# Selective-state mixer and expert layer on one core: projecting B and C before the output, and taking the key/query norm's power before a block's deviation

## The reference, cut to what matters

```
Bn = B * rsqrt(mean(B*B) + 1e-5) * B_norm_w          # C alike
K  = rope(Bn + B_bias, theta)   # 4 heads x 128; Q from C, theta = cumsum(angles * dt)
y_intra = (Q K^T * decay mask) @ x ;  y_inter = Q @ state ;  state = fade*state + K^T x
out = ((y_intra + y_inter + D*x) * silu(z)) @ W_out
```

## Time and profile before

| | |
|---|---|
| median of 3 runs | 280.01 us (279.19 to 280.21) |
| profiled execution | 278.36 us, span 276.6 us |
| TensorE busy | 248.3 us (90%) |
| VectorE busy | 223.8 us (81%) |
| GpSimd busy | 208.3 us (75%) |
| ScalarE busy | 149.2 us (54%) |
| granted TensorE clock, mean | 0.969 |

### The profile page before, as it was taken

One profiled execution on the slowest core, in us unless ns is written; L12 is line 12 of the kernel. 1 busy time (PEld: TensorE's weight loads), 2 busy tenths in 40 slices (PEclk: granted clock), 3 DMA queues, 4 the chain that ended last, 5 costly groups with the idle time before them and its releaser, 6 DMA issues.

```text
span 276.6 us, 7390 instructions
## 1 busy us (share of the span) xinstructions
PE 248.3 (90%) x2155; PEld 218.4 (79%) x2158; DVE 223.8 (81%) x607; ACT 149.2 (54%) x508; POOL 208.3 (75%) x291
## 2 busy tenths in 40 slices
PE   2999997599999999999999999999999999999600
PEld 0857964488997999899889979997999899889400
DVE  4768998988878969896989698788969896987446
ACT  1765989555365453745364645456453755372033
POOL 8658997858788888788887888888788876675400
PEclk9999999799999999999999999999999999999955
DMA  5540827976869888987897688969878997770096
GB/s 157 195 129 11 298 86 219 303 202 207 265 192 270 275 246 239 289 264 208 261 293 263 216 248 262 316 196 269 276 239 253 275 268 248 231 236 21 21 274 181
DMA packets 68855, 61.55 MB, mean 222 GB/s; under 512 B 6608, under 2 KB 52304, under 8 KB 68816
## 3 DMA queue, kind: packets, MB, share of 16 engines
q1 hardware_dynamic: 66256, 55.83, 66.3%
q0 software_dynamic: 2560, 5.25, 6.3%
HBM read 56.27 MB, written 4.78 MB: 221 GB/s over the span
## 4 chain that ended last, share of the span: by engine, by line
PE 72%; DVE 10%; ACT 6%; POOL 4%; DMA 3%; issue 3%; SPq 1%; POOLq 0%; ACTq 0%; DVEq 0%
PE bank L877 20%; PE bank L922 9%; PE bank L872 5%; PE bank L820 5%; PE bank L812 5%; PE bank L836 3%; PE bank L797 3%; PE bank L767 3%; PE bank L804 2%; PE bank L772 2%; PE bank L854 2%; PE bank L845 2%; PE bank L918 2%; DMA decay<-res_dram 2%; PE bank L863 2%
## 5 line engine op out<-in xcount | busy, mean ns | idle before, releaser
L877 PE MATMUL bank<-blkT,w_up 128*128 128x128 f32 x512 | 64.4, 279 | 1.2 <-ACT blkT L1091 1.2
L877 PEld LDWEIGHTS bank<-blkT,w_up 128*128 128x128 f32 x512 | 61.8, 195 | 2.0 <-issue 1.3
L637 POOL DMA_INDIRECT res_dram<-xrow,sidx x40 | 40.7, 1018 | 22.0 <-DVE xrow L1423 17.7
L583 POOL DMA_INDIRECT blk<-xn_dram,gidx x40 | 42.1, 1052 | 8.7 <-issue 7.6
L922 PE MATMUL bank<-w,xrow 128*128 128x128 f32 x256 | 34.7, 278 | 0.3 <-DVE xrow L1410 0.3
L922 PEld LDWEIGHTS bank<-w,xrow 128*128 128x128 f32 x256 | 31.1, 192 | 1.6 <-issue 1.6
L1327 DVE SCALAR_TENSOR_TENSOR kq<-sd,rms,bias_kq 128x512 f32<-128x512 f32 x32 | 23.5, 772 | 10.6 <-POOL rms L594 9.8
L1097 ACT ACTIVATE xrow<-bank 128x512 f32<-128x512 f32 x40 | 24.6, 614 | 13.6 <-PE bank L877 13.6
L1395 DVE TENSOR_TENSOR xrow<-xrow,bank 128x512 f32<-128x512 f32 x40 | 27.1, 678 | 0.6 <-PE bank L877 0.6
L630 POOL TENSOR_TENSOR rstd<-mv,mhalf 128x1 f32<-128x1 f32 x40 | 25.2, 629 | 1.5 <-DVE mv L1407 1.3
L1060 ACT ACTIVATE kqT<-bank 128x512 f32<-128x512 f32 x16 | 9.6, 597 | 27.3 <-PE bank L797 27.3
(11 more groups left out here) (246 smaller groups left out, 620.6 us busy)
## 6 DMA issues: line engine op xcount, KB each, us to landing
w_up<-in_L_ffn_W_dram SPq DMA_DIRECT2D x96, 256.0 KB
w<-in_L_ffn_W_dram SPq DMA_DIRECT2D x48, 256.0 KB, 4.4
e_row<-e_dram SPq DMA_DIRECT2D x16, 256.0 KB, 4.2
decay<-l_dram SPq DMA_DIRECT2D x4, 512.0 KB, 5.5
gam<-in_L_ffn_gamma_dram SPq DMA_DIRECT2D x32, 64.0 KB
shift_y<-in_L_ffn_beta_dram SPq DMA_DIRECT2D x32, 64.0 KB
acc<-in_L_attn_u_dram SPq DMA_DIRECT2D x4, 256.0 KB, 3.8
xn_dram<-xrow SPq DMA_DIRECT2D x4, 256.0 KB, 5.6
```

Of the source, the lines that this page charges most:

```text
L583: g.indirect_dma_start(out=blk[:, b % SLOTS, :], out_offset=None, in_=xn_dram, in_offset=bass.IndirectOffsetOnAxis(ap=gidx[:, entry(b):ent ...
L637: g.indirect_dma_start(out=res_dram, in_=res[:, b % HALF, :], in_offset=None, out_offset=bass.IndirectOffsetOnAxis(ap=sidx[:, entry(b):ent ...
L877: last = m(bank[out][:, c * P:(c + 1) * P], w_up[:, u % SETS, n, c * P:(c + 1) * P], blkT[:, b % 2, :], start=True, stop=True)
```

## The change

Three reorderings; no instruction is added or dropped. On TensorE, `project_bc(t)` goes ahead of `project_out(t-2)`. On VectorE, `mean_square(t)` and `weigh_bc(t)` go ahead of `add_out(t-2)`. On GpSimd, `rms_pow(t)` goes ahead of `finish(b0-2)`.

```
 # GpSimd
             def iteration(t, first, second, blocks):
                 b0, b1, b2 = blocks
-                if b0 is not None:
-                    finish(b0 - 2)
                 if first and t > 0:
                     rms_pow(t)
                 if b0 is not None:
+                    finish(b0 - 2)
                     gather(b0 + SLOTS)
 # TensorE
                 if ends_:
                     down(b0 - 1)
+                if first and not begins:
+                    project_bc(t)
                 if t >= 2:
                     project_out(t - 2)
-                if first and not begins:
-                    project_bc(t)
 # VectorE
+                if first and not begins:
+                    mean_square(t)
+                    weigh_bc(t)
                 if t >= 2:
                     add_out(t - 2)
                 if first and not begins:
-                    mean_square(t)
-                    weigh_bc(t)
                     norm_kq(t)
```

## The result

| | before | after |
|---|---|---|
| median of 7 runs each, taken together | 279.19 us (278.54 to 280.48) | 276.85 us (276.48 to 278.04) |
| profiled execution | 278.36 us | 276.62 us |
| span | 276.6 us | 274.8 us |

The ratio of the changed kernel to the kernel before is 0.9912, 95% interval 0.9895 to 0.9929: 0.88% faster, between 0.7% and 1.05%. The predicted time was 277.9 us. The three runs behind the old median of 280.01 are among the seven that now give 279.19.

A forecast was written before the change was run, and what follows sets the result against it. TensorE was taken as the fullest engine, losing 0.30 us per even iteration waiting for VectorE. The terms 1.26 + 0.02 + 0.63 + 0.20 = 2.11 us, off the median 280.01, gave 277.9 us, range 277.1 to 280.2.

The forecast's parts named there:

- From the median: 280.01 - 2.11 = 277.9: Whole kernel: the summed gain of 2.11 us taken off the old median of 280.01 us, 0.75% less.
- `norm_kq`'s start: VectorE in even iterations: `norm_kq` starts 0.55 us earlier, its hole falls from 0.66 to about 0.4, L1327 keeps 1.47.
- K's load, 6 x 0.21: TensorE, K's weight load waiting for `rotate`: 0.21 us saved in each of six even iterations, 1.26 us.
- `carry`, 7 x 0.09: TensorE, state product's weight load waiting for `carry` in even iterations: 0.09 us saved seven times, 0.63; likely, not read.
- t = 1, 0.20: TensorE in t = 1: a weight load's 0.20 us wait for VectorE's product goes entirely.
- All three edits are needed for the 0.55: Even iterations: without `project_bc` earlier, `mean_square` would hold `rms_pow` and leave 0.21 of the 0.55 us.
- 0.55 us is more than the 0.21 and the 0.09: Even iterations: VectorE's 0.55 us lead exceeds what TensorE lacks, so `rotate` and `carry` end early enough and the wait goes.
- The products behind the swap: TensorE behind the reordered products: length change taken as zero; at most +3.5 us, or -0.8 if it drains faster.
- locked out: Rival, VectorE beside GpSimd: `finish` holds `norm_kq` until 129.65 as now, TensorE's waits stay; 280.0 us, chance 0.20.
- TensorE bound: Rival, TensorE busy 188.72 of 189.00 us: distances are structure and the order moves nothing; 280.0 us, chance 0.03.
- the half case: Rival: `carry`'s 0.09 us are TensorE's own pace and t = 1 gives less; gain 1.28 us, 278.7 us, chance 0.18.
- The slower case: Rival, odd iterations: L1311 shifts against GpSimd's `weigh_q` (L622) and costs 1.81 us; +2.3 us, 282.3 us, chance 0.07.

The follow-up runs named there:

- experiments 1: Kernel before with only TensorE's and VectorE's reorderings, GpSimd's order kept: 279.58 us, ratio to the kernel before 1.001.
- experiment 4: Changed kernel with VectorE's `gate_y` ahead of `fade` and `carry` in even iterations too, making `carry` late: 278.65 us, ratio to the kernel before 0.9991.
- 7: Changed kernel plus an idle 256-column VectorE operation ahead of `norm_kq` in even iterations: 278.12 us, ratio to the kernel before 0.9938.
- 8: Changed kernel plus an idle 512-column VectorE operation ahead of `norm_kq` in even iterations: 278.07 us, ratio to the kernel before 0.9951.
- 11: Kernel before with one other edit, GpSimd's `square_own` directly behind `rot_sine`, ahead of `store(b0-2)`: 277.93 us, ratio to the kernel before 0.9949.
- Experiment 3: Kernel before with TensorE's and GpSimd's reorderings, VectorE's order kept: 277.24 us, ratio to the kernel before 0.9931.
- 2: Kernel before with only GpSimd's reordering: 279.29 us, ratio to the kernel before 1.000.
- experiment 9: Changed kernel with `weigh_q(15)` between the last two powers at the end of GpSimd's list, and stores behind both: 277.39 us, ratio to the kernel before 0.992.
- 10: Changed kernel with `weigh_q(15)` behind both last powers and stores at the end of GpSimd's list: 276.40 us, ratio to the kernel before 0.9914.
- 12: Changed kernel with `square_own` directly behind `rot_sine` and `weigh_q` behind the last powers and stores: 276.39 us, ratio to the kernel before 0.9899.
- 5: Kernel before with one other edit, GpSimd's `square_own` behind `finish` and `gather` of b1: 279.87 us, ratio to the kernel before 1.0005.

## Why the prediction was right, and where it failed

**The mechanism and its sum held.** K's load waits no longer, and experiments 1, 4, 7, 8 and 11 show that this wait and the carry's are what the change removes. The profiled execution went from 278.36 to 276.62 where 276.25 was forecast, and the medians taken together differ by 2.34 us where the sum said 2.11. That the terms seen in the trace also add up to 2.34 is chance: the trace lost 0.35 and 0.2 of that again, and the interval of the ratio runs from 2.0 to 2.9 us.

**The step that failed is the level: "From the median: 280.01 - 2.11 = 277.9".** The median of three runs was a poor level. Seven runs of the kernel before gave 279.19, 35 others 279.35, and single ones of these lay between 278.46 and 280.76; the profiled execution, 1.65 us lower, was itself a fair sign. The range carried this on: its low end was 280.01 less 2.9, and for spread it allowed 0.2 us, upward only. From 279.19 the same sum gives 277.08, just outside it already, and the same bounds give a range from 276.29 on, which holds the measured 276.85. The other 0.2 are the sizes below.

- **`norm_kq`'s start**: 0.55 us earlier, as predicted; its hole 0.37 against 0.4, its pair 1.42 against 1.47.
- **K's load, 6 x 0.21**: mis-sized. The 0.60 of an odd iteration holds 0.17 from L862 to L796; an even one without a wait has 0.11 (121.02 - 120.85 against 134.79 - 134.68). The odd reference stands behind a mixed block's narrow tiles, and the even one does not; that the tiles cost these 0.06 is likely, and no run isolates it. So the part is 0.27 where it is whole; t = 2 got less (below).
- **`carry`, 7 x 0.09**: right in t = 4 to 12 (1.37 to 1.27), and experiment 4 shows `carry` as its cause. In t = 2 it stayed, since `carry` still ended 10.04 us behind L766, against 9.83 in t = 6: that iteration gained 0.24.
- **t = 1, 0.20**: 0.11. `norm_kq` started only 0.20 us earlier there.
- **"All three edits are needed for the 0.55"**: wrong. Experiment 3 has the gain without VectorE's edit. `add_out` takes 0.28 us, and the hole before `norm_kq` covers it wherever it stands. Experiments 1 and 2 show that the other two are both needed. In 2, I had 0.21 us of the 0.55 left without TensorE's edit, and no part of it reached `rotate`.
- **"0.55 us is more than the 0.21 and the 0.09"**: held, but by less than I wrote, and by another path. I took VectorE for one chain from `mean_square` to `carry`. The rows show that `rotate` hangs on GpSimd: `rot_sine` starts 0.46 us earlier than before, directly behind a gather that did not move (3.44 us behind L766 against 3.48), `square_own` 0.47 and `rotate` 0.46. I had `rotate` end 0.33 us before the load; the lead is 0.19, and 7 and 8 show that about 0.13 us of lateness is free.
- **The products behind the swap**: no cost and no gain, as taken; odd iterations keep 14.43 to 14.45 us.
- **The rivals**: locked out is refuted (L1326 1.42 beside L630). The Trainium skill, "SBUF — State Buffer", section "Who interferes with whom", has a VectorE instruction with two SBUF inputs and a GpSimd instruction that reads SBUF exclude each other. These traces do not agree for a power on one element per partition, and agree for GpSimd's product of whole tiles: L1310 took 2.49 us and ended 0.56 us behind L622 (the prediction had its own length, 0.68), and `shift_block` took 1.36 us in experiment 9. TensorE bound is refuted by experiments 1 and 11, and the half case by the balance. The slower case did not come: L1310 and L622 kept 0.79 us between their starts in t = 5 (111.02 and 111.81).

Two things are open. The pause of 0.35 us in t = 11 has no named cause; 3, 9, 10 and 12 do not show it there, and 11 has a like one in t = 5. And the spread between runs was not taken apart, since each kernel has one trace. Between the traces the first L766 of the loop starts at 60.13 to 62.59 us, and the stretch behind L766 of t = 15 takes 35.3 to 37.1 us. The wait for the first gathered block (4.0 to 6.8 us) does not decide the start alone: with 4.01 and with 4.84 it was 60.14, with 4.14 it was 61.17.

## What to carry to other kernels

Where the bounding engine waits a little in a fixed place, its releaser's chain is worth exactly the wait and no more: find how late the releaser is. Here every edit tried that took that much out of its chain removed the wait (two swaps, or one other swap), and more was worth nothing. Whether the edit costs as much elsewhere, as in 5, only a run tells. Follow the chain through every engine: here VectorE's product ended with an operation of GpSimd that it does not wait for. Compare an iteration with its wait against an identical one without, not against one that has other neighbours. And take the level from more than three runs, or give the range the profiled execution's distance from their median.

## What the runs showed of the hardware

- A VectorE product of two 256-column SBUF tiles takes 0.42 us alone and 0.69 to 0.90 where GpSimd's 512-column mask (`square_own`) starts beside it; the mask itself takes 0.69 to 0.73 instead of 0.64. The first of two such products ended 0.18 to 0.23 us behind the mask's start, however early it had started. Both products of `rot_cosine` paid this in the kernel before, about 0.7 us an iteration, more than the 0.55 us by which the change moved `norm_kq`.
- VectorE is not slowed by GpSimd's power on a 128x1 tile: L1326's pair takes 1.41 or 1.42 us with a power of 0.53 us beside it, and 1.41 to 1.48 without. The power on a 128x2 tile never ran beside a VectorE operation with two SBUF inputs.
- K's transposes start 0.17 us behind L862 in odd iterations, where a mixed block's narrow tiles stand ahead of it, and 0.11 in even ones, where full tiles do.
- TensorE's wait for the first gathered block varied from 4.0 to 6.8 us between these kernels' traces, which differ only behind it, but for one fill of a scratch tile in 7 and 8.
